# f2 with both parts of W_proj side by side and its halves summed by VectorE, with four jobs moved, in a transformer block on one Trainium2 core

## The reference

```python
x = x + attn(layernorm(x))          # linear attention, 16 heads of 64
#   q = elu(xn @ Wq) + 1;  k = elu(xn @ Wk) + 1;  v = xn @ Wv
#   z = q . sum_n(k) + 1e-6;  kv = sum_n(k^T v);  out = (q @ kv / z) @ Wo + bo
x = x + ffn(layernorm(x))
#   h = square(relu(xn @ W_fc^T));  y = h @ W_proj^T            (1024 wide inside)
#   five spiking steps on y, all with the same input y:
#   mem = 0.9*mem + y - (mem > 1);  spk = (mem > 1);  result = sum(spk) / 5
```

## Time and profile before

| | |
|---|---|
| median of three runs | 1033.61 us |
| the profiled execution | 1033.73 us, of it 1031.9 us span |
| PE busy | 1024.2 us (99%) |
| DVE busy | 883.9 us (86%) |
| ACT busy | 742.2 us (72%) |
| POOL busy | 662.8 us (64%) |
| chain that ended last | PE 98%, DVE 1% |
| granted clock of PE | 1.00 over the span |

### The profile page before, as it was taken

The page is one execution under the profiler, slowest core; times in us unless marked ns, Lnnn a source line. Parts: engine busy times, 40 slices in busy tenths (PEclk is TensorE's granted clock), DMA queues, the critical chain, the costliest instruction groups (busy, mean ns, idle before and its releaser), DMA issues.

```text
span 1031.9 us, 19936 instructions
## 1 busy us (share of the span) xinstructions
PE 1024.2 (99%) x7063; PEld 655.0 (63%) x7063; DVE 883.9 (86%) x1877; ACT 742.2 (72%) x1228; POOL 662.8 (64%) x414
## 2 busy tenths in 40 slices
PE   8999999999999999999999999999999999999998
PEld 4444444444444467776777767777777777777887
DVE  7899888898889699999898898888888888888875
ACT  8788787767867749676777767676767676776664
POOL 1444354465447479677687776878677877777835
PEclk9999999999999999999999999999999999999999
DMA  4546543334324545435354444545454445444331
GB/s 133 148 127 145 118 119 94 80 69 117 92 73 94 121 79 113 94 91 109 88 126 106 91 105 88 115 96 106 94 113 98 102 94 111 105 96 89 78 81 44
DMA packets 265173, 104.24 MB, mean 101 GB/s; under 512 B 219249, under 2 KB 262513, under 8 KB 265073
## 3 DMA queue, kind: packets, MB, share of 16 engines
q1 hardware_dynamic: 264928, 102.90, 44.4%
q10 hardware_dynamic: 144, 0.07, 0.0%
HBM read 33.69 MB, written 16.79 MB: 49 GB/s over the span
## 4 chain that ended last, share of the span: by engine, by line
PE 98%; DVE 1%; DMA 0%; ACT 0%; issue 0%; ACTq 0%; DVEq 0%
PE proj L650 32%; PE acc L819 16%; PE acc L855 16%; PE acc L696 16%; PE acc L794 8%; PE acc L796 4%; PE acc L803 4%; PE proj L718 1%; PE proj L731 1%; PE acc L756 0%; PE acc L664 0%; DMA xT<-xnat 0%; PE proj L707 0%; DMA x_t<-in_L_attn_x_dram 0%; DVE xn L1448 0%
## 5 line engine op out<-in xcount | busy, mean ns | idle before, releaser
L910 ACT ACTIVATE feat<-proj 128x1024 f32<-128x1024 f32 (+1 forms) x125 | 126.0, 1008 | 186.0 <-PE proj L650 185.7
L1656 POOL TENSOR_TENSOR h<-h_f,h 128x512 f16<-128x512 f32 x128 | 148.8, 1183 | 161.4 <-ACT h L1103 161.4
L1615 POOL TENSOR_TENSOR qT<-qT,feat 128x1024 f32<-128x1024 f32 x60 | 142.4, 2374 | 162.5 <-DVE xnat L1239 143.2
L819 PE MATMUL acc<-xn2T,wfcT 128*128 128x256 f16 x1536 | 178.0, 273 | 0.0
L855 PE MATMUL acc<-wpT,h 128*128 128x256 f16 (+1 forms) x1560 | 177.9, 271 | 0.1
L696 PE MATMUL acc<-feat,xnat 128*128 128x512 f16 x768 | 176.2, 379 | 0.0
L650 PE MATMUL proj<-wk,xT 128*128 128x512 f16 x756 | 173.4, 379 | 0.2 <-DMA xT<-xnat 0.2
L819 PEld LDWEIGHTS acc<-xn2T,wfcT 128*128 128x128 f16 x1536 | 150.3, 98 | 28.9
L1621 POOL TENSOR_TENSOR feat<-feat,rz 128x1024 f32<-128x1024 f32 x60 | 164.7, 2745 | 4.5 <-DVE rz L1351 4.5
L650 PE MATMUL proj<-wq,xT 128*128 128x512 f16 x720 | 165.3, 379 | 0.0
L855 PEld LDWEIGHTS acc<-wpT,h 128*128 128x128 f16 x1560 | 150.6, 98 | 22.6 <-issue 0.3
(11 more groups left out here) (118 smaller groups left out, 1339.4 us busy)
## 6 DMA issues: line engine op xcount, KB each, us to landing
x_t<-in_L_attn_x_dram SPq DMA_DIRECT2D x128, 128.0 KB, 2.3
xT_spill<-xT SPq DMA_DIRECT2D x64, 128.0 KB, 2.1
out_dram<-out_t SPq DMA_DIRECT2D x63, 128.0 KB, 2.1
xT<-xT_spill SPq DMA_DIRECT2D x60, 128.0 KB, 2.3
ks_all<-ks_rows SPq DMA_DIRECT2D x4, 512.0 KB, 4.1
qT<-feat SPq DMA_TRANSPOSE x120, 3.1
m_all<-in_L_attn_Wk_dram SPq DMA_DIRECT2D x4, 256.0 KB, 4.5
xT<-xnat SPq DMA_TRANSPOSE x64, 2.4
```

The lines of the kernel that those rows point to most:

```text
L819: mm = pe.matmul(acc[:, 2 + g % 2, f % 2 * 2 * P:(f % 2 + 1) * 2 * P], wfcT[:, left, f * C2 + c2, :], xn2T[:, pair % 4, right * C2 + c2, : ...
L1615: pool.tensor_tensor(kacc[:, b % 2, :], kacc[:, b % 2, :], k_feat(n), ALU.add).then_inc(k_added, 1)
L1656: pool.tensor_tensor(lo, h_f[:, k % 4, :], hi, ALU.subtract).then_inc(h_lo, 1)
```

## The change

Three parts.

1. In the first phase q of tile 2 goes from place 44 to 41, the kv split of batch 2 from 56 to 61, two of the weight splits one place earlier (20 to 19, 21 to 20, 22 to 21), and Wo is loaded before Wv.
2. `f2_tile` of tiles 8 to 55 takes the form of `o_tile`: eight matmuls of 512 columns into the whole bank 1, eight of 256 into its left half. ACT copies the right half to SBUF (`take_right`, at the start of its step, ahead of the exp of q). DVE adds it to the left half into `y_sum`, also in SBUF, just ahead of the first threshold step; the five threshold steps of these tiles then read `y_sum`. The next `f2_tile` waits for that sum (`y_summed`) and no longer for the five steps. Both buffers lie in the low part of Wk, which nobody needs in the second phase.
3. Of tile 57, the first `f1_group` goes from step 64 to the step before, ahead of f2 of tile 54.

```diff
+        y_sum = wk[:, LO, 0, 0:2 * D].bitcast(F32)
+        y_right = wk[:, LO, 1, 0:2 * D].bitcast(F32)
...
-                  36: ("kv", 1, 0), 44: ("q", 2), 49: ("q", 3), 52: ("kv", 2, 0)}
+                  36: ("kv", 1, 0), 41: ("q", 2), 49: ("q", 3), 52: ("kv", 2, 0)}
-        KV_SPLITS = {22: 0, 40: 1, 56: 2}
+        KV_SPLITS = {22: 0, 40: 1, 61: 2}
...
-        SPLIT_AT = {n: PIECES[4 + i] for i, n in enumerate((5, 6, 7, 8, 9, 10, 11, 12, 13, 14, 15, 18, 20, 21, 22, 23))}
+        SPLIT_AT = {n: PIECES[4 + i] for i, n in enumerate((5, 6, 7, 8, 9, 10, 11, 12, 13, 14, 15, 18, 19, 20, 21, 23))}
...
-            for i, w in enumerate(("proj", "q", "v", "o")):
+            for i, w in enumerate(("proj", "q", "o", "v")):
...
                 before = n - (n > TILES - 6)
-                wait_past(pe, spike_steps, 5 * min(before, HALVED))
+                if before - 1 in WIDE:
+                    pe.wait_ge(y_summed, WIDE.index(before - 1) + 1)
+                else:
+                    wait_past(pe, spike_steps, 5 * min(before, HALVED))
...
-                for half in range(2 if n == TILES - 1 else 1):
+                if n in WIDE:
+                    for f in range(FB):
+                        pe.matmul(acc[:, 1, :], h[:, pair % 2, HI, f, u * P:(u + 1) * P], wpT[:, :, f::FB, :],
+                                  start=(f == 0), stop=(f == FB - 1), skip_group_check=True)
+                        mm = pe.matmul(y_at(n), h[:, pair % 2, LO, f, u * P:(u + 1) * P], wpT[:, HI, f::FB, :],
+                                       start=False, stop=(f == FB - 1), skip_group_check=True)
+                    mm.then_inc(f2_done, 1)
+                for half in range(0 if n in WIDE else 2 if n == TILES - 1 else 1):
...
-                    f1_half(n)
+                    if t == TILES:
+                        f1_group(blocks_of(n)[1])
+                    else:
+                        f1_half(n)
                 for n in at(o_step, t):
                     o_tile(n)
+                if t == TILES - 1:
+                    for n in at(f1_step, t + 1):
+                        f1_group(blocks_of(n)[0])
...
+            def take_right(n):
+                act.wait_ge(f2_done, n + 1)
+                wait_past(act, y_summed, WIDE.index(n))
+                act.activation(y_right, acc[:, 1, D:2 * D], ACT.Copy).then_inc(y_right_taken, 1)
...
+                for n in at(f2_step, t - 1):
+                    if n in WIDE:
+                        take_right(n)
...
+                if n in WIDE:
+                    y = y_sum
+                    if k == 0:
+                        dve.wait_ge(f2_done, n + 1)
+                        dve.wait_ge(spike_steps, 5 * n)
+                        dve.wait_ge(y_right_taken, WIDE.index(n) + 1)
+                        dve.tensor_tensor(y, acc[:, 1, 0:D], y_right, ALU.add).then_inc(y_summed, 1)
+                        dve.wait_ge(y_summed, WIDE.index(n) + 1)
```

More of the change, by code:

```diff
@@ L195, in build @@
         shares = sem("shares")
+        y_right_taken, y_summed = sem("y_right_taken"), sem("y_summed")
         out_ready = sem("out_ready")
```

## The result

The changed kernel takes 1112.41 us (median of 4 runs, 1112.19 to 1113.51), the one before 1033.47: a ratio of 1.0766 (95% interval 1.0752 to 1.0779), 78.9 us slower. The prediction was 1132, slower, with a range of 1070 to 1158.

The account below looks back on a forecast made before the run. PE was taken as the bound until DVE's standing for POOL exceeds 4.5 us a pair; 24 pairs x 4.17 = 100 us, less 0.8 and 0.4, added to 1033.6 gives 1132 us, range 1070 to 1158.

Parts of the forecast that it names:

- The bound and the rule: PE, busy 99%, bounds the kernel; a DVE instruction with two SBUF operands and a POOL instruction exclude each other.
- The first rival: DVE's standing for POOL stays under 4.5 us a pair, so PE stays the bound: 1032.4 us, no change; 8%.
- the room: In two second-phase steps of 20.86 us, DVE can stand 4.5 us for POOL before the pair gets longer.
- standing of DVE in two steps: DVE waiting for POOL in the threshold steps, L1336 and the write, laid out by turns: 8.65 us together.
- DVE's own work in two steps: DVE's work without standing in a second-phase pair: 16.4 us, 7.4 in the even tile's step and 9.0 in the other.
- wide f2: f2 on PE, eight matmuls fewer a tile for equal columns: 0.8 us gained over 48 tiles, 0.5 to 1.4.
- jobs and f1 group: Moved jobs and f1 group remove PE standstills before 330.57 and 974.98: 0.4 us gained, bounds 0.7 either way.
- The layout: DVE and POOL taking turns by whole instructions from an even tile's residual: 8.65 us standing, pair 25.0 us, 4.17 more.
- the reading of L1228: DVE's tensor_scalar with its tensor in SBUF takes 1.22 us beside POOL, so the first threshold step excludes POOL too.
- The other signs: Expected traces: many threshold steps of 1 to 2.3 us, PE idle some 4 us before every second o, PE near 90%.
- the case above 1153: Slower than forecast: PE stands some 4 us every second step, and a granted clock under 1.00 adds PE time; 6%.
- The case of the write: The write after step five gets ahead of POOL's L1621: standing 6.78 us, 1087 us; with surroundings 1064 to 1093, 12%.

## Why the prediction was right, and where its sizes were off

**The bound and the rule** held. PE gives 0.8 us at most; what moves the time is DVE standing for POOL. The copy alone in SBUF brings 78.5 us of 78.9, PSUM for that one operand takes 78 back, and a shorter instruction of POOL takes back all of it. The first rival (little standing, no change) is what the cut low part of q shows: the room is real. By the measured own work it is 20.86 - 16.7 = 4.2 us, for the 4.5 laid out.

**The terms.**

| term | predicted | measured |
|---|---|---|
| standing of DVE in two steps | 8.65 us | 7.6 us |
| DVE's own work in two steps | 16.4 us | 24.27 - 7.6 = 16.7 us |
| two steps | 25.0 us | 24.27 us |
| 24 pairs above 20.86 us each | +100 us | 3.41 us in the pair shown; 574.97 - 496.79 = +78.2 us over all 24 |
| wide f2 | -0.8 us | -0.9 us by starts, where PE is the bound |
| jobs and f1 group | -0.4 us | -0.5 us, in the run with these alone |
| the whole | +98.8 us | +78.9 us |

The 574.97 and 496.79 us run from the first step of tile 8 to that of tile 56 (497.17 to 1072.14, and 496.73 to 993.52 before). Not every pair is like the one shown: in the changed kernel the first eight take 23.2 to 27.0 us, the next twelve 24.24 to 24.27, and the last four 23.8, 23.8, 27.0 and 14.0 (the last was 13.0 before).

The term that was mis-sized is the standing, laid out turn by turn, by 1.0 us, or 25 us of time. The layout failed in two places. At its start it let POOL's two low parts of h begin with the residual of DVE; in the changed kernel they begin 1.36 us before it (688.03 against 689.39), so POOL's low part of q is done at 692.6, just as the first step comes, and that step, which I had at 1.27, stands next to nothing in the step shown. And it took the small scaling of z (L1372) as free of POOL; it stands 1.93 us for POOL's low part of q. While it stands, the inverse of z behind it is late, so POOL has nothing to do for 0.60 us (waiting for it), and steps 4 and 5, which I had at 1.00 and 1.93, meet no instruction of POOL. The write stands 1.58 for my 1.87, and the two L1261 of the other step 0.95 for none. Which instruction stands is thus a matter of tenths. That the total came within 1.0 us is in part luck: 4.2 us of standing that I laid out (steps 1, 4 and 5) did not come, and 3.8 us that I did not lay out (step 3, L1372 and L1261) did.

The second miss is small and goes the other way: I took 0.30 us from start to start for a step from SBUF, by the shortest L1434, where it is 0.34 from either place. So steps 2 to 5 gain nothing; only the first (duration 0.30 for 0.42) does. That is 0.3 us in two steps, 7 us.

A rough check: 1132 - 25 + 7 = 1114, against 1112.

One step of the reading of L1228 is weaker than it was put. In the earlier trace rows DVE's start is recorded 0.03 us before POOL's, and yet it is DVE that stood: at so small a distance the recorded starts do not tell who asked first.

**The other signs.** L1463 with many values of 1 to 2.2 us, the write up to 2232 ns, DVE hardly idle before the residual (L1522: 2.9 us over the 48 wide tiles, 53.6 before), PE standing before o every second step: as foretold (3.1 us for "some 4"). The steps take 14.98 and 9.29 us in turn (691.96, 706.94, 716.23), not 10.4 and 14.6; that sign did not follow from the layout, which had 16.0 and 9.0. Medians of the step stay at 0.42, as most of them still meet nothing. PE is at 94%, not 90: matmuls at a lower clock count as busy for longer. That clock is what I named in the case above 1153. In stretches of 50 us from 500 us on the granted clock is now 0.93 to 1.00 where it was 1.00, and two o tiles near the end take 4.45 us for 2.78, just after PE stood 3.7 and 4.2 us:

```profile
1043.35 4.45 PE L806 MATMUL acc<-m_all,qT 128*128 128x256 f16 x24 [3.71 <-DVE x L1526]
...
1057.19 4.45 PE L806 MATMUL acc<-m_all,qT 128*128 128x256 f16 x24 [4.18 <-DVE x L1526]
```

The view by stretches gives these two (busy time of PE, PEld, DVE, ACT and POOL, then the granted clock) a mean of 0.60, so most of each runs at the lower level, 1.2 GHz:

```profile
1043.35:1047.60 4.25, 4.25 (x24) 3.19 (x25) 4.18 (x13) 3.44 (x10) 0.72 (x1) 0.60 0.74 167
1057.10:1061.40 4.30, 4.21 (x24) 3.16 (x25) 4.16 (x6) 2.10 (x5) 4.20 (x3) 0.60 0.59 104
```

DVE is busy there too (4.18 of 4.25 us). What the clock adds to the time can be read from two pairs of steps that differ in it, the pair read above and one further on:

```profile
691.96:716.23 24.27, 21.14 (x138) 13.16 (x137) 23.92 (x41) 14.73 (x27) 15.53 (x11) 1.00 0.42 88
861.80:886.05 24.25, 21.24 (x117) 12.07 (x116) 23.91 (x41) 13.21 (x25) 15.51 (x11) 0.86 0.42 88
```

At 1.00 and 0.86 the pair takes the same: PE's slower matmuls fall into time in which it would have stood (before o at 753.18 it stands 1.61 us, where it stands 3.02 at 728.91), and DVE sets the time. So in these steps the clock adds nothing. For the long pairs at both ends (27.0 us, at 0.87 and 0.94) its part was not separated.

**The case of the write** (through ahead of POOL's next instruction) didn't occur in the steps shown. The Trainium skill ("VectorE: DVE Perf Modes", section "Rules for kernel authors") offers copying from PSUM to SBUF first, when many operations follow, beside simply reading PSUM; for this kernel the run with the copy alone speaks against the copy, 78.5 us slower. The rule of the lock in the Trainium skill ("SBUF — State Buffer", section "SBUF: two separate sides") is borne out: 361 to 2176 ns for the step with two SBUF operands, 381 to 426 with one in PSUM.

**What stays open.** The sum in PSUM and f2's wait for the fifth step give two levels, 2 to 4 us apart, in two of three measurements. PE's only new standstills in the low executions are before f2 near 974 and 982 us, 0.2 to 0.5 us each; no trace of a high execution exists, so where it loses is not shown. In the run without the moved jobs six of the seven high executions have a mean granted clock of 0.998 and the low ones 0.999 or 1.00; in the first run with the sum in PSUM the nine high ones have 0.999 or 1.00 as well, so a lower clock does not account for both.

## What to carry to other kernels

An operand's place is part of an instruction's price: before moving an operand of a VectorE instruction from PSUM to SBUF, see whether all its tensor operands would then lie in SBUF (a TENSOR_SCALAR with its only one there was held too, up to 1.88 us for step 1 in the run with the copy) and what GpSimd does at that moment. Look for it inside the durations (one line with a minimum of 0.4 and a maximum of 2.2 us), since no wait and no idle time shows it. The cost is a threshold: compare the sum of the standing in a period with the idle time that VectorE has in it; two of five steps cost 6 or 34 us here, by where they stand in the order (and, in part, by the kind of the first).

## What was not expected of the hardware

- A TENSOR_SCALAR of VectorE on 128x16 fp32 elements in SBUF, with one tensor operand, takes 0.16 us alone and up to 2.10 us when it stands for GpSimd (157 to 2097 ns in the changed kernel). The TENSOR_REDUCE over 128x1024 in SBUF was never held in 60 cases (1.20 to 1.22 us).
- A SCALAR_TENSOR_TENSOR on 128x256 fp32 that nothing holds takes the same from two SBUF operands (0.34 us from start to start; 361 ns the shortest duration) as from PSUM and SBUF (0.34 us; 379 ns).
- When one instruction of GpSimd was cut from 128x1024 to 128x128 (2.1 to 0.43 us a tile), the kernel, in which TensorE was idle for want of VectorE, became 79 us faster.
- TensorE's granted clock fell to a mean of 0.86 over two steps without making them longer, because TensorE was not the bound there (24.25 us against 24.27).
